# Gated cross-attention block: keys and queries projected once, their threefold rows made by DMA through DRAM, and a new order of the turn

## What is computed

```python
x = x + tanh(g_xattn) * attention(layernorm(x), ctx, ctx, mask)      # 16 heads of 8 features
x = x + tanh(g_ffn)   * mixture(layernorm(x))                        # 8 experts, 128 -> 512 -> 128
# attention: q = x Wq' + bq, k = ctx Wk' + bk, v = ctx Wv' + bv
# scores = q k' / sqrt(8), masked; softmax; times v; times Wo' + bo
```

## Time and profile before

| what | value |
|---|---|
| median of 3 runs | 689.93 us (689.4 to 690.32) |
| the profiled execution's own time | 691.63 us |
| its span | 689.8 us |
| granted TensorE clock over the span | 0.981 |
| busy share: TensorE (PE), VectorE (DVE), ScalarE (ACT), GpSimd (POOL) | 92%, 77%, 63%, 27% |
| mean DMA rate | 76 GB/s |

### The profile page before, as it was taken

How to read it: one execution, slowest core, us unless ns; L and a number is a source line. 1 busy time by engine, 2 the same in 40 slices (tenths; PEclk the granted TensorE clock), 3 DMA queues, 4 the chain that set the end, 5 groups by cost and what they waited for, 6 DMA issues and landing times.

```text
span 689.8 us, 14449 instructions
## 1 busy us (share of the span) xinstructions
PE 635.0 (92%) x3944; PEld 479.0 (69%) x3944; DVE 534.3 (77%) x1083; ACT 432.7 (63%) x764; POOL 188.1 (27%) x242
## 2 busy tenths in 40 slices
PE   2899999999999998829999999999999999999996
PEld 2566666666666666427878878878778788787784
DVE  5778888888888887544877877868868778688686
ACT  3466666666666665517757757757577677675773
POOL 6224344444433342110130220221302202212022
PEclk9999999999999999958999999999999999999999
DMA  6544344444444434102121121121111211111110
GB/s 191 135 118 121 104 115 116 113 111 117 111 110 110 110 104 104 57 0 69 46 62 48 46 62 48 46 47 61 53 54 46 61 46 46 46 61 48 58 46 15
DMA packets 48139, 52.74 MB, mean 76 GB/s; under 512 B 9329, under 2 KB 34801, under 8 KB 48113
## 3 DMA queue, kind: packets, MB, share of 16 engines
q1 hardware_dynamic: 48112, 52.42, 27.8%
HBM read 26.58 MB, written 2.23 MB: 42 GB/s over the span
## 4 chain that ended last, share of the span: by engine, by line
PE 79%; DVE 8%; issue 3%; POOL 3%; DMA 3%; SPq 2%; ACT 2%; DVEq 0%; POOLq 0%; ACTq 0%
PE ps_y L1040 8%; PE ps_y L1042 8%; PE ps_y L1041 8%; PE ps_h L1062 8%; PE ps_h L1060 8%; PE ps_h L1061 8%; PE scores L993 5%; PE scores L994 4%; PE scores L1001 4%; PE scores L1002 3%; POOL yT L527 3%; DVE neg_max L654 3%; PE heads L1012 3%; PE misc L881 2%; PE misc L882 2%
## 5 line engine op out<-in xcount | busy, mean ns | idle before, releaser
L627 ACT ACTIVATE h_sb<-ps_h,b_sb 128x512 f32<-128x512 f32 x256 | 175.3, 689 | 116.0 <-PE ps_h L1062 103.3
L840 DVE TENSOR_TENSOR h_low<-h_sb,h_high 128x512 fp32r<-128x512 f32 x256 | 164.4, 682 | 0.0
L527 POOL TENSOR_TENSOR yT<-yT,weighted 128x512 f32<-128x512 f32 x56 | 72.3, 1291 | 308.9 <-DVE weighted L828 308.2
L836 DVE CAST h_high<-h_sb 128x512 fp32r<-128x512 f32 x128 | 87.0, 679 | 81.4 <-ACT h_sb L627 81.3
L1040 PE MATMUL ps_y<-h_high,w_high 128*128 128x512 f32 x256 | 102.0, 399 | 4.9 <-DVE h_low L840 4.9
L1060 PE MATMUL ps_h<-x_high,w_high 128*128 (+1 forms) x256 | 101.7, 397 | 0.0
L1042 PE MATMUL ps_y<-h_high,w_low 128*128 128x512 f32 x256 | 101.4, 396 | 0.0
L1062 PE MATMUL ps_h<-x_high,w_low 128*128 (+1 forms) x256 | 101.2, 395 | 0.0
L1041 PE MATMUL ps_y<-h_low,w_high 128*128 128x512 f32 x256 | 100.7, 393 | 0.0
L1061 PE MATMUL ps_h<-x_low,w_high 128*128 (+1 forms) x256 | 100.1, 391 | 0.0
L654 DVE TENSOR_REDUCE neg_max<-scores 128x4 f32<-128x512 f32 x128 | 83.7, 685 | 14.2 <-PE scores L1002 13.1
(11 more groups left out here) (122 smaller groups left out, 989.6 us busy)
## 6 DMA issues: line engine op xcount, KB each, us to landing
w_row<-w_scratch SPq DMA_DIRECT2D x64, 256.0 KB, 3.2
k_masked<-k_stack SPq DMA_DIRECT2D x64, 128.0 KB, 2.5
k_cur<-k_stack SPq DMA_DIRECT2D x16, 512.0 KB, 3.1
q_masked<-q_stack SPq DMA_DIRECT2D x64, 96.0 KB
w_raw<-in_w_ffn SPq DMA_DIRECT2D x16, 256.0 KB, 2.7
ctx_sb<-in_ctx SPq DMA_DIRECT2D x16, 128.0 KB, 2.1
out_y<-y_out SPq DMA_DIRECT2D x8, 256.0 KB, 3.6
probs<-in_wqk SPq DMA_DIRECT2D x2, 256.0 KB, 2.9
```

Of the source, the lines that this page charges most:

```text
L527: nc.gpsimd.tensor_tensor(yT[:], yT[:], weighted[:, e % 2, :], ALU.add).then_inc(added, 1)
L627: nc.scalar.activation(h_sb[:, j % HBUF, :], ps_h[:, j % 4, :], ACT.Gelu_apprx_tanh, bias=b1_sb[:, j:j + 1]).then_inc(h_done, 1)
L840: V.tensor_tensor(h_low[:, j % HBUF, :], h_sb[:, j % HBUF, :], h_high[:, j % HBUF, :].bitcast(F32), ALU.subtract).then_inc(low2_done, 1)
```

## The change

Keys and queries are each projected once: 128 dense rows, high and low weights, 6 matmuls of 256 columns a turn. ScalarE rounds the result to `kq_high`, VectorE writes the remainder `kq_low`. Six DMAs a turn store these in a DRAM scratch, the high part twice and the low part once for each of keys and queries, in the threefold order. Ten DMAs load from there: `q_stack` (96 rows), `k_masked` (four of 24 rows), `q_masked` (four of 24 rows) and `k_cur` (96 rows). The maxima now stand in rows 96 and 97. The tensors `k_stack` and `part` are gone, and with them the eight `part` operations and the eight of `stacks`. The bias is loaded by eight small DMAs near the start, in place of two.

The pipeline is two turns longer (`FIRST`, `LAST`): inputs and projection run three groups ahead, not two; `merged`, `wo` run a turn later, the second norm's transposition and the gate two turns later than `heads`. PE's order in a turn, before: P4, T02, P6, v, T03, T10, inputs, V00, V01, T11, N00, N01, T12, T13, N02, x2T, N03, V10, V11, N10, max0, N11, heads, P0, N12, N13, merged, P2, gate, T00, max1, T01, wo (P is a `project`, V a `values`). After: T02, V00, merged, T03, N00, T10, N01, T11, N02, T12, N03, T13, N10, V01, N11, max0, wo, N12, V10, V11, N13, x2T, inputs, v, gate, max1, T00, heads, T01, kq. The other engines' bodies are laid out to match. ACT copies the first maximum ahead of its other work; DVE writes `kq_low` ahead of its reductions.

The core of the diff (SP's body with its new order stands whole):

```diff
-BANKS = [["p45", "inputs", "x2T", "p01"],
-         ["p67", "max0", "p23"],
-         ["v", "heads", "merged", "gate", "wo"]]
-AHEAD = {"p45": 1, "p67": 1, "v": 1, "inputs": 2, "x2T": -1, "max0": 1, "heads": 0,
-         "p01": 2, "merged": 0, "p23": 2, "gate": -1, "wo": 0}
-FIRST, LAST = -3, NG
-STEADY = (2, NG - 3)
+BANKS = [["wo", "inputs", "kq"],
+         ["merged", "max0", "x2T", "gate", "heads"],
+         ["v"]]
+AHEAD = {"wo": -1, "inputs": 3, "kq": 3, "merged": -1, "max0": 1, "x2T": -2, "gate": -2, "heads": 0, "v": 2}
+FIRST, LAST = -4, NG + 1
+STEADY = (2, NG - 4)
+KROWS = 3 * ROWS * HD
...
+        k_masked = sa("k_masked", [P, ROWS, SLABS, GT], F32R)
+        q_masked = sa("q_masked", [P, ROWS, SLABS, GT], F32R)
         q_stack = sa("q_stack", [P, SLABS, GT], F32R)
         k_cur = sa("k_cur", [P, SLABS, GT], F32R)
+        kq_high = sa("kq_high", [P, 2, GT], F32R)
+        kq_low = sa("kq_low", [P, 2, GT], F32R)
...
+        kq_dram = nc.dram_tensor("kq_scratch", (NG, 2, KROWS, SLABS * GT), F32)
...
+            bias_v = a["bqk"].rearrange("(r c d) (n s) -> n c r d s", r=ROWS, c=COMBOS, s=SLABS)
+            for r in range(ROWS):
+                for n in range(2):
+                    sp.dma_start(bkq[4 * HD * r:4 * HD * (r + 1), n:n + 1], bias_v[n, 0, r]).then_inc(bias_in, 16)
...
-                sp.dma_start(q_masked[24:26, :, :, b * S:(b + 1) * S].rearrange("p s r q -> p (s r) q").bitcast(F32),
+                sp.dma_start(q_masked[KROWS:KROWS + 2, :, :, b * S:(b + 1) * S].rearrange("p r s q -> p (r s) q").bitcast(F32),
                              maxT[:, b * S:(b + 1) * S].bitcast(F32)).then_inc(max_in[b], 16)
...
+            high_v = kq_dram[:].rearrange("g n (r c d) (s t) -> g n c r (d s) t", r=ROWS, c=3, t=GT)
+            def store(n, c, src, g, done):
+                sp.dma_start(of_group(high_v, g)[:, n, c].rearrange("g r p t -> (g r) p t"),
+                             src[:, n, :].bitcast(F32)).then_inc(done, 16)
+            def load(dst, n, rows, g):
+                return sp.dma_start(dst.bitcast(F32), of_group(kq_dram[:], g)[:, n, rows, :].rearrange("g p x -> (g p) x"))
             def body(it):
+                if (g := group_at(it, 2)) is not None:
+                    if not first(g):
+                        sp.wait_ge(masknxt_done, g)
+                        settle(sp)
+                        sp.wait_ge(maskcur_done, g)
+                        settle(sp)
+                        sp.dma_start(mask_words[:], of_group(mask_v, g)).then_inc(mask_in, 16)
+                    sp.wait_ge(high_stored, g * 64 + 64)
                     settle(sp)
+                    sp.wait_ge(low_stored, g * 32 + 32)
                     settle(sp)
+                    if first(g):
+                        sp.wait_ge(pad_done, 3)
                     else:
                         sp.wait_ge(scoresN_full[1], fill_of(g - 1, GB - 1, SLABS - 1))
                         settle(sp)
+                    load(q_stack[0:KROWS, :, :].rearrange("p s t -> p (s t)"), 1, slice(0, KROWS), g).then_inc(qs_in, 16)
                     for r in range(ROWS):
+                        rows = slice(3 * HD * r, 3 * HD * (r + 1))
+                        load(k_masked[rows, r, :, :].rearrange("p s t -> p (s t)"), 0, rows, g).then_inc(km_in, 16)
+                if (g := group_at(it, 1)) is not None:
+                    sp.wait_ge(maxT1_done, g + 1)
                     settle(sp)
+                    if not first(g):
+                        sp.wait_ge(scoresT_full[1], fill_of(g - 1, GB - 1, SLABS - 1))
+                        settle(sp)
+                    max_rows(1)
+                if (g := group_at(it, 2)) is not None and not first(g):
+                    sp.wait_ge(wsplit_done, g)
                     settle(sp)
+                    sp.dma_start(w_raw[:], of_group(a["w_ffn"], g).rearrange("g p x -> (g p) x")).then_inc(w_in, 16)
+                if (g := group_at(it, 4)) is not None and not first(g):
+                    misc_wait_full(sp, "inputs", g - 1)
                     settle(sp)
+                    sp.dma_start(ctx_sb[:], of_group(ctx_v, g).rearrange("g p b d -> (g p) b d")).then_inc(ctx_in, 16)
+                if (g := group_at(it, 3)) is not None:
+                    sp.wait_ge(kq_high_done, g + 1)
+                    settle(sp)
+                    for n, c in ((0, 0), (0, 2), (1, 0), (1, 1)):
+                        store(n, c, kq_high, g, high_stored)
+                    misc_wait_read(sp, "kq", g)
+                    settle(sp)
+                    for n, c in ((0, 1), (1, 2)):
+                        store(n, c, kq_low, g, low_stored)
+                if (g := group_at(it, 2)) is not None:
+                    if not first(g):
                         sp.wait_ge(scoresT_full[1], fill_of(g - 1, GB - 1, SLABS - 1))
                         settle(sp)
                     for r in range(ROWS):
+                        rows = slice(3 * HD * r, 3 * HD * (r + 1))
+                        load(q_masked[rows, r, :, :].rearrange("p s t -> p (s t)"), 1, rows, g).then_inc(qm_in, 16)
+                    load(k_cur[0:KROWS, :, :].rearrange("p s t -> p (s t)"), 0, slice(0, KROWS), g).then_inc(kcur_in, 16)
+                    misc_wait_read(sp, "max0", g)
                     settle(sp)
                     max_rows(0)
...
+                    misc_wait_full(act, "kq", g)
+                    wait_count(act, high_stored, g * 64)
+                    for n in range(2):
+                        ins = nc.scalar.activation(kq_high[:, n, :], misc[:, bank_of("kq"), n * GT:(n + 1) * GT], ACT.Identity,
+                                                   bias=bkq[:, n:n + 1])
+                    ins.then_inc(kq_high_done, 1)
...
+                    dve.wait_ge(kq_high_done, g + 1)
+                    wait_count(dve, low_stored, g * 32)
+                    for n in range(2):
+                        ins = nc.vector.scalar_tensor_tensor(kq_low[:, n, :], misc[:, bank_of("kq"), n * GT:(n + 1) * GT], bkq[:, n:n + 1],
+                                                             kq_high[:, n, :].bitcast(F32), ALU.add, ALU.subtract)
+                    ins.then_inc(misc_read[bank_of("kq")], 1)
...
+                    misc_wait_read(pe, "inputs", g)
+                    misc_wait_free(pe, "kq", g)
+                    for n in range(2):
+                        dst = misc[:, bank_of("kq"), n * GT:(n + 1) * GT]
+                        src_h, src_l = inT_high[:, n * GT:(n + 1) * GT], inT_low[:, n * GT:(n + 1) * GT]
+                        mm(dst, wqk_high[:, n, :], src_h, start=True, stop=False)
+                        mm(dst, wqk_high[:, n, :], src_l, start=False, stop=False)
+                        ins = mm(dst, wqk_low[:, n, :], src_h, start=False, stop=True)
+                    ins.then_inc(misc_full[bank_of("kq")], 1)
 
...
-                mm(dst, k_cur[:, s, b * S:(b + 1) * S], q_masked[:, s, :, b * S:(b + 1) * S], start=True, stop=False)
+                mm(dst, k_cur[0:KROWS + 2, s, b * S:(b + 1) * S], q_masked[0:KROWS + 2, :, s, b * S:(b + 1) * S], start=True, stop=False)
...
-                mm(dst, q_stack[:, s, b * S:(b + 1) * S], k_masked[:, s, :, b * S:(b + 1) * S], start=True, stop=False)
+                mm(dst, q_stack[0:KROWS, s, b * S:(b + 1) * S], k_masked[0:KROWS, :, s, b * S:(b + 1) * S], start=True, stop=False)
```

More of the change, by code:

```diff
@@ L549, in body @@
             def body(it):
-                def parts(i, g):
-                    what = f"p{i}{i + 1}"
-                    misc_wait_full(act, what, it)
-                    if i >= SLABS:
-                        misc_wait_read(act, f"p{i - 4}{i - 3}", it - 1)
-                    elif not (isinstance(g, int) and g == 0):
-                        misc_wait_read(act, f"p{i + 4}{i + 5}", it)
-                    for k in range(2):
-                        nc.scalar.activation(part[:, (i + k) % 4, :], misc[:, bank_of(what), k * GT:(k + 1) * GT], ACT.Identity,
-                                             scale=low_rows[:, i + k:i + k + 1],
-                                             bias=bqk_low[:, i + k:i + k + 1]).then_inc(part_done, 1)
+                if (g := group_at(it, 0)) is not None:
+                    exp_slab(g, 1, 2)
@@ new lines, in body @@
+                if (g := group_at(it, -1)) is not None:
+                    if isinstance(g, int) and g == 0:
+                        pe.wait_ge(wts_in, N_WTS)
+                    misc_wait_read(pe, "merged", g)
+                    misc_wait_free(pe, "wo", g)
+                    for b in range(GB):
+                        ins = mm(misc[:, bank_of("wo"), b * D:(b + 1) * D], mergedT[:, b * S:(b + 1) * S], wo_sb[:], start=True, stop=True)
+                    ins.then_inc(misc_full[bank_of("wo")], 1)
@@ L958, in body @@
-                if (g := group_at(it, 0)) is not None:
-                    misc_wait_read(pe, "heads", it)
```

(18 more changed lines are left out.)

455 lines of the change are left out of this document (205 added, 250 removed).

## The result

The changed kernel takes 764.5 us (median; 761.44 to 766.02), the kernel before 689.77 us (689.4 to 690.32): a ratio of 1.1076, 95% interval 1.1046 to 1.1107. The profiled execution took 765.05 us, with a span of 763.3 us and a mean granted clock of 0.919.

What follows compares the result with a forecast made beforehand. PE's work bounds the kernel now; afterwards the chain through stores on four engines sets an 18.5 us turn. 15 x (18.5 - 16.8) = 25.5 plus 14 at the start gives +40, 730 us; range 668 to 775.

Steps and rivals of the forecast that it cites:

- PE, ACT, DVE: Engine work per turn: PE down 2.1 us to 14.7, ACT 3.4 less, DVE 2.9 less to 12.0; ACT and DVE don't bind.
- The engines of a store: Scratch stores: target's outermost number is 4, so each runs on 4 DMA engines, the same four for all six.
- The price of a packet: Scratch stores: 50 ns per 1 KB packet, 40 and 75 kept; 9.6 us a turn on four engines (7.7 to 14.4).
- Rival (b): Scratch stores on four engines but at 40 ns a packet, so SP's queue rules: +15, 705 us; chance 0.15.
- The chain of a turn: From kq's end through roundings, stores, loads, maxima, landing and PE's pieces to kq: sum 18.2, with waits 18.5 us.
- rival (c): Packets at 75 ns (805 us), or PE's clock falls behind a 4 us stop (turn 20.6, 761 us); chance 0.18.
- the central sum: Whole kernel: 15 turns x (18.5 - 16.8) = 25.5, plus 14 at the start: +40 us, 730 us; chance 0.45.
- SP's queue: SP's DMA issues, waits and gaps in a turn: 12.6 + 2.6 + 1.7, thus 16.9 us (bounds 15 and 18.5).
- Rival (a): Stores spread over 16 engines or are taken in stride: turn 15.2, start +6, 672 us; chance 0.22.
- The start: Before the first turns: early bias loads 2.5 us, then about 11 us between kq and N00: +14 us.
- Chances and range: Total time: slower 0.75, faster 0.22, within 0.2% 0.03; range 668 to 775 us, the forecast's own 712 to 752.

Runs made afterwards that it cites:

- the last kernel: Changed kernel with the store target's cut reordered, three loads issued by ScalarE in better places, and one bias DMA in place of eight: 674.12 us, ratio 0.9766.
- the reordered kernel: Changed kernel with scratch, weight and bias rows ordered (feature, slab, head), so a store's target is cut 32 x 4 x 256: 689.87 us, ratio 1.0004.

## Why the prediction was right, and where it was off

**PE, ACT, DVE.** Right. PE's 14.3 us at full clock (the last kernel) stand against 14.7; DVE's 12.1 against 12.0. Both gains lay beside the chain.

**The engines of a store.** Right: share 0.25, 2061 packets against 2060 worked out for four, the same four for all six stores (97 GB/s throughout), and 75 us when the cut alone is changed. The Trainium skill's rule (DMA: Bandwidth & Descriptors, section "Why a DMA increments its semaphore by 16 and not by 1"), the largest engine count up to 16 that divides the slowest dimension of both sides, is borne out by these runs in count. Its other half, that these are always the lowest-numbered engines, fits six stores that never move more than 97 GB/s together; the engines' numbers are seen in no row.

**The price of a packet.** 42 ns where the stores are alone, 50 to 57 in the turn, against 50 taken and 40 to 75 kept. Rival (b)'s 40 ns is not what a turn has.

**The chain of a turn.** Predicted 16.1 us without PE's part: measured 20.56 - 4.0 = 16.5. Of it, the roundings and the wait behind them 1.1 us (157.72 to 158.81) against 1.3; from the first store's issue to T00 15.4 us (158.81 to 174.18) against 1.0 + 9.6 + 2.8 + 0.45 + 0.9 = 14.75. The step that failed is the last term, "then T00, heads, T01 and kq on PE, 2.1": it is 4.0 us, because the clock stood at 0.50 after the stop. I had named it in rival (c), with a turn of 20.6 and 761 us, at a chance that it shared with dear packets, 0.18; measured are 20.56 and 764.5. The mechanism of the forecast and the clock's half of (c) came true together. The stop of nearly 4 us was itself part of the forecast, showed what follows such a stop, and so this half of (c) belonged in the central sum: 15 x (20.6 - 18.5) = 31 us of the 34.5 that were missing. No run gives all of that back: with the stop filled 13 us came, and SP's wait for `w_raw` took part of the rest.

**SP's queue.** Too dear in the forecast. "About 0.65" for a 24-row load is 0.45 for `k_masked` (1.78 for four) and 0.70 for `q_masked` (2.81 for four), whose issues stand behind the narrow stores; with stores on 16 engines these too are short (1.79 in the last kernel). The 96-row loads are 0.32 against 0.40. A store is 0.75 with its gap, against 0.78. The eleven rows of a turn sum to 12.2 us, gaps within a group included, against 12.6 + 1.7 (the terms written down for the 12.6 add up to 12.7); with 13 waits at 0.2 that is 14.8 of a turn of 20.5, so SP stood idle, and rival (b), SP as the bound, was no case with the stores on four engines. Rival (a) did not occur, but the reordered kernel is its experiment: turn 15.87 against 15.2, total 689.87 against 672, since the start was 10.2 us later, not 6, and the old steady turns of 16.8 were only 0.9 longer. With SP relieved and one bias DMA, 674.12.

**The start.** Predicted +14, measured +18.5 at the first `k_cur`. The timeline of SP has the cause of a part of it:

```profile
3.20 5.86 SPq L354 DMA_DIRECT2D bkq<-in_bqk  x8
```

Eight small DMAs at 0.73 us push `kq` from 12.18 to 16.33 us, 4.1 in place of 2.5. From `kq` to N00 it is then 21.1 us against 9.7 before, 11.4 more, as predicted (11); the other 3 us are the second group's stores before T00, which the prediction left to its range.

**Chances and range.** 764.5 lies in 668 to 775, and slower had 0.75; but the forecast's own 712 to 752 did not hold it, and a range that takes in 3% faster as well as 12% slower says little. That the time fell inside it owes more to its width than to the sum.

## What to carry to other kernels

Before a DMA with a rearranged DRAM side is added, look at its outermost extent on both sides: here 4 in place of 32 made 128 rows run on four engines and cost 75 us, and reordering rows that no one else reads took it back. When a forecast contains a stop of PE of several us that recurs, price the work behind it at half clock in the central sum (here 4.0 us in place of 2.1, in 15 turns). A load moved in a queue changes what stands behind it and what waits for it: 779.69 us came with `w_raw` put ahead of the loads that PE waits for, 720.33 with a mask that was late for GpSimd, 677.57 with the same three loads of the latter in better places. And read a stop together with the ring that it is part of: it can shrink while the work behind it starts no sooner.

## What was not expected of the hardware

The granted clock fell in every turn in spite of PE's 16 us of work in 20.5: with stops of 4.8 us the mean clock of a turn is 0.83, and it is 1.00 in the two turns shown of the last kernel, whose stops are near 1 us. A 24-row load from DRAM takes 0.45 us to issue where the 24-row copy between SBUF tensors took 0.85; small bias loads at the start took 0.73 each. And a second queue helped little: with the loads for T00 issued by ScalarE `k_cur` still took 6.4 us to land while SP's stores ran on four engines, against 3.9 from SP's own queue with stores on 16.
